# Selective scan: seven of 64 weightings by C moved from VectorE to GpSimd

## What is computed

```python
def _L3_attn_ref(x, norm_w, W_skip, W_in, conv_w, conv_b, Wd1, Wd2, bd2, WB, WC, A_log, W_D, W_out):
    B, L, D = (4, 256, 256)
    E, N, DT, DC = (512, 16, 128, 4)
    ...
    delta = jax.nn.softplus(u @ Wd1.T @ Wd2.T + bd2)
    Bt = u @ WB.T
    Ct = u @ WC.T
    A = -jnp.exp(A_log)

    def step(h, inps):
        d_l, b_l, c_l, u_l = inps
        h = jnp.exp(d_l[..., None] * A) * h + (d_l * u_l)[..., None] * b_l[:, None, :]
        y_l = jnp.einsum('ben,bn->be', h, c_l)
        return (h, y_l)
    ...
    y = (y + u * W_D) * jax.nn.silu(skip)
    return y @ W_out.T
```

## Time and profile before

| what | value |
|---|---|
| median of 3 executions | 1641.8 us (1636.6 to 1643.69) |
| the profiled execution, its own time | 1640.15 us |
| its span, first to last instruction | 1638.8 us |
| busy over the span | PE 1488.8, DVE 1206.6, ACT 895.7, POOL 373.6 us |
| first scan of the loop starts | 1165.06 us |
| last scan of the loop starts | 1387.71 us |
| mean granted TensorE clock | 0.967 |

### The profile page before, as it was taken

The page is one execution under the profiler, slowest core; times in us unless marked ns, Lnnn a source line. Parts: engine busy times, 40 slices in busy tenths (PEclk is TensorE's granted clock), DMA queues, the critical chain, the costliest instruction groups (busy, mean ns, idle before and its releaser), DMA issues.

```text
span 1638.8 us, 16560 instructions
## 1 busy us (share of the span) xinstructions
PE 1488.8 (91%) x5269; PEld 815.9 (50%) x5280; DVE 1206.6 (74%) x1970; ACT 895.7 (55%) x1612; POOL 373.6 (23%) x239
## 2 busy tenths in 40 slices
PE   6898999999799999988999999767888888999998
PEld 2565465478444444344555555333233333467776
DVE  8586587557556367588898988686899999656565
ACT  6444377355323213468888878476766534244443
POOL 1000432241101001000000000020488876023232
PEclk9999999999899999999999999987899999999999
DMA  4001594360300000222121212102000000111110
GB/s 135 1 1 36 228 323 158 83 121 1 154 0 0 0 16 1 66 49 68 26 75 24 75 25 71 59 1 84 0 1 0 1 0 0 55 38 49 55 44 27
DMA packets 45799, 88.19 MB, mean 54 GB/s; under 512 B 10064, under 2 KB 27408, under 8 KB 43408
## 3 DMA queue, kind: packets, MB, share of 16 engines
q1 hardware_dynamic: 40624, 61.42, 12.6%
q0 software_dynamic: 5088, 25.69, 4.3%
HBM read 70.43 MB, written 7.22 MB: 47 GB/s over the span
## 4 chain that ended last, share of the span: by engine, by line
PE 34%; DVE 9%; ACT 6%; issue 4%; POOL 4%; PEldq 1%; DMA 0%; POOLq 0%; DVEq 0%; SPq 0%; ACTq 0%; PEld 0%
PE bank L159 25%; PE bank L3273 3%; POOL s_bu L3168 3%; DVE s_bu L2988 2%; PE bank L2513 2%; DVE s_bu L2983 1%; PE bank L2489 1%; PE bank L3199 1%; DVE g_p L2160 1%; PE bank L2500 1%; DVE g_th L2179 1%; PEldq L147 1%; POOL q_t L2736 1%; PE bank L2488 0%; ACT g_p L2326 0%
## 5 line engine op out<-in xcount | busy, mean ns | idle before, releaser
L3168 POOL TENSOR_TENSOR s_bu<-s_rep,s_du 128x1024 f32<-128x1024 f32 x64 | 150.8, 2361 | 92.8 <-ACT s_rep L3036 54.4
L2983 DVE TENSOR_TENSOR_SCAN s_bu<-bank,s_bu 128x1024 f32<-128x1024 f32 x64 | 146.5, 2288 | 4.7 <-POOL s_bu L3168 2.7
L159 PE MATMUL bank<-e_xs,e_wsp 128*128 128x512 f32 x528 | 127.7, 391 | 0.7 <-issue 0.7
L3273 PE MATMUL bank<-s_bu,ident 128*128 128x512 f32 x256 | 124.7, 610 | 0.7 <-DVE s_dl L2940 0.2
L3052 ACT ACTIVATE bank<-s_dl,s_an 128x510 f32<-128x510 f32 x128 | 82.8, 683 | 53.1 <-DVE s_bu L2983 53.1
L2736 POOL TENSOR_TENSOR q_t<-q_t,q_g 128x704 f32<-128x704 f32 x8 | 13.8, 1720 | 428.9 <-ACT q_t L2781 428.9
L159 PEld LDWEIGHTS bank<-e_xs,e_wsp 128*128 128x128 f32 x528 | 99.1, 188 | 22.7 <-issue 1.9
L159 PE MATMUL bank<-r_am,r_b 128*128 128x512 f32 x240 | 106.0, 592 | 1.4 <-DVE r_am L1783 1.4
L159 PE MATMUL bank<-conditioned,g_wqk 128*128 128x512 f32 x160 | 79.8, 624 | 8.0 <-ACT g_th L2351 7.8
L1849 ACT ACTIVATE r_sl<-bank 128x512 f32<-128x512 f32 x28 | 16.7, 597 | 128.7 <-PE bank L159 128.7
L3383 DVE TENSOR_TENSOR e_s<-e_s,bank 128x512 f32<-128x512 f32 (+1 forms) x50 | 34.3, 686 | 68.8 <-ACT e_s L3515 68.8
(11 more groups left out here) (530 smaller groups left out, 3587.2 us busy)
## 6 DMA issues: line engine op xcount, KB each, us to landing
g_turn<-g_q SPq DMA_DIRECT2D x64, 128.0 KB, 2.3
e_wgu<-in_e_gu SPq DMA_DIRECT2D x22, 256.0 KB, 2.7
b_vw<-b_values SPq DMA_DIRECT2D x48, 64.0 KB, 3.1
e_wd<-in_e_down SPq DMA_DIRECT2D x22, 128.0 KB, 2.6
r_w<-in_r_w SPq DMA_DIRECT2D x3, 896.0 KB, 9.1
g_wqk<-in_g_qk SPq DMA_DIRECT2D x4, 640.0 KB, 4.0
g_wgv<-in_g_gv SPq DMA_DIRECT2D x4, 640.0 KB, 3.9
g_wo<-in_g_wo SPq DMA_DIRECT2D x4, 512.0 KB, 3.9
```

The costliest lines, as they stand in the source:

```text
L159: last = e.matmul(out, lhs, rhs, start=start and n == 0, stop=stop and n == len(pairs) - 1, skip_group_check=True)
L2983: e.tensor_tensor_scan(b, flat(k.pairs[n % 2][:, :, :]), b, 0.0, ALU.mult, ALU.add).then_inc(k["s_scanned"].up(), 1)
L3168: e.tensor_tensor(m.bu[n % m.NBU][:, :, :], m.rep[:, 2 * np:2 * np + 2, :], m.du[:, et, half(h)].unsqueeze(1).to_broadcast([P, 2, HALF]), ...
L3273: summed = e.matmul(banks[6][:, :], k.ident[:, :], m.bu[(n - 1) % m.NBU][:, i, :], start=np == 0 and i == 0, stop=np == m.NP - 1 and i == ...
```

## The change

For the seven jobs in `LATE` (11, 19, 27, 35, 43, 51, 59) VectorE's weighting is left out. ScalarE copies the spread rows of C of that job from `pairs[2]` to an SBUF tile, `kept()` (the space of `s_rs`, [128, 2, 512]), behind decays of the job two further on. GpSimd multiplies `bu` by that tile, in place, behind the input of the job two further on. TensorE's next spread waits for the copy (`spread_free`) and its sum waits for the late weighting (`weighted`).

```diff
+    LATE = [11, 19, 27, 35, 43, 51, 59]
+
+    def kept(self):
+        return self.rs[:, :].rearrange("p (i t) -> p i t", i=2)
+
+    def weighted(self, k, n):
+
+        late = sum(x <= n for x in self.LATE)
+        return k["s_weighted_late"].at(late) if n in self.LATE else k["s_weighted"].at(n + 1 - late)
+
+    def spread_free(self, k, n):
+
+        late = sum(x <= n for x in self.LATE)
+        return k["s_spread_kept"].at(late) if n in self.LATE else k["s_weighted"].at(n + 1 - late)
...
@@ selective_vector
-        if n >= 1:
+        if n >= 1 and n - 1 not in m.LATE:
...
@@ selective_scalar
+        if n - 2 in m.LATE:
+            x = m.LATE.index(n - 2)
+            e.wait_ge(*k["s_spread_c"].at(n - 1))
+            if x:
+                e.wait_ge(*k["s_weighted_late"].at(x))
+            e.copy(flat(m.kept()), flat(k.pairs[2][:, :, :])).then_inc(k["s_spread_kept"].up(), 1)
...
@@ selective_pool
+        if n - 2 in m.LATE:
+            b = m.bu[(n - 2) % m.NBU][:, :, :]
+            e.wait_ge(*k["s_scanned"].at(n - 1))
+            e.wait_ge(*k["s_spread_kept"].at(m.LATE.index(n - 2) + 1))
+            e.tensor_tensor(b, b, m.kept(), ALU.mult).then_inc(k["s_weighted_late"].up(), 1)
...
@@ selective_tensor
-                e.wait_ge(*k["s_weighted"].at(n))
+                e.wait_ge(*m.spread_free(k, n - 1))
...
-            e.wait_ge(*k["s_weighted"].at(n))
+            e.wait_ge(*m.weighted(k, n - 1))
```

## The result

Over seven executions each, the change took 1647.26 us at the median (1645.84 to 1650.85) and the kernel before 1637.81 (1634.78 to 1643.69). The ratio is **1.0056, with a 95% interval of 1.0039 to 1.0074**: slower by 9.2 us, between 6.4 and 12.1. The profiled execution of the change took 1646.19 us with a span of 1644.5, against 1640.15 and 1638.8.

A forecast was written before the change was run, and what follows sets the result against it. VectorE was taken to bound the loop, at GpSimd's pace where GpSimd has no gap. Seven places summed to +7.1 us: 1647.3 from the profiled 1640.15, 1648.9 from the median, forecast 1648.0, range 1640 to 1656.

The forecast's parts named there:

- VectorE bounds the loop, GpSimd's lead decides: Loop: VectorE busy 218.44 of 227 us; cost set by time from GpSimd's input end to scan start, 0.1 to 1.6 us.
- Relief 7.8 us at most, waited away but at job 43: VectorE: seven weightings of 1.11 us removed, 7.8 us at most; job 43 forecast at -0.8 us.
- Copy 1.00, late product 2.36 us: Each late job: ScalarE's copy out of PSUM takes 1.00 us, GpSimd's 128 x 1024 product 2.36 us.
- Copy on ScalarE costs nothing: ScalarE, idle for nearly half of the loop: the seven copies' own time costs nothing; only when they end counts.
- The copy ends behind decays(L+2): ScalarE at late job L: the copy follows decays(L+2); at job 59 it ends near 1379.0, before GpSimd finishes input(61).
- Job 11, +2.3: At scan(14): GpSimd has no lead, so the late product is paid whole, +2.3 us.
- TensorE costed at nothing: TensorE's moved waits for copy and late weighting: 0 us, since it has room, busy 191 of 227 us.
- the second rival: TensorE's clock falls in its new waits, one to seven falls adding 0.7 to 5 us: 1651 us, chance 0.15.
- The first: GpSimd takes the product in its slack, all 7.8 us of VectorE's time come out: 1632.4 us, chance 0.05.
- The third: Shared SBUF read port: each late product holds a scan up 2.3 us, 16 in all: 1663 us, chance 0.03.
- The fourth: It comes out even: lead rebuilt ahead of scans 24 and 38, job 27 caught up by 34: 1640 to 1643, chance 0.15.

The follow-up runs named there:

- e1: The change with GpSimd's late product cut to columns 0 to 15 of each state, copies and waits kept: 188.63 us from scan(8) to scan(63), ratio 1.0003.
- e4: The change with late jobs 11, 27 and 35 only: 199.41 us from scan(8) to scan(63), ratio to the kernel before 1.0040.
- e11: The change with VectorE weighting all 64 jobs again; copies, full-length late products and TensorE's waits kept: 204.61 us from scan(8) to scan(63), ratio 1.0076.
- e3: The kernel before plus seven ScalarE copies and TensorE's next spread waiting for them, no GpSimd product: 192.08 us from scan(8) to scan(63), ratio 1.0002.
- e10: The change with six buffers, late product and its sum one place back, late jobs 16, 36, 41, 44, 57: 188.09 us from scan(8) to scan(63), ratio 0.9975.
- e7: The change, same seven late jobs, with six bu buffers in place of four: 200.21 us from scan(8) to scan(63), ratio 1.0046.
- e9: The change, same seven late jobs, with six buffers, late product and its sum one place back: 200.84 us from scan(8) to scan(63), ratio 1.0049.
- e2: The change with VectorE weighting all 64 jobs, GpSimd multiplying the kept tile by itself, result unused: 197.84 us from scan(8) to scan(63), ratio 1.0040.
- e12: The same kernel as e10, profiled and timed again: 188.49 us from scan(8) to scan(63), ratio to the kernel before 0.9978.
- e6: The kernel before with six bu buffers in place of four: 191.38 us from scan(8) to scan(63), ratio 1.0001.
- e8: The change with six buffers, late product and its sum one place back, late jobs 17, 36, 41, 44, 50, 57: 188.84 us, ratio 0.9978.

## Why the prediction was right

The forecast was +7.1 us, from the profiled execution to 1647.3 and from the median to 1648.9, given as 1648.0. Measured were +9.2 by the ratio (6.4 to 12.1), +7.2 in the loop from scan(8) on, and 1647.26 us. The two totals lie closer than the two differences do, since the kernel before came out lower in the seven runs, 1637.81, than in the three shown; so far the nearness of 1648.0 to 1647.26 is luck. So is some of the agreement of +7.1 with +7.2: job 11 came out 1.6 us cheaper than forecast, and this was made up by 0.8 at scans 30 to 34 and 0.2 to 0.3 each at jobs 19, 51 and 59. I gave the larger chance, 0.55, to a change within 0.5%; 1.0056 lies just outside, and its interval reaches over that bound to both sides.

- **VectorE bounds the loop, GpSimd's lead decides.** Right. e1 shows that GpSimd's 2.3 us are the price, and e4 that they cost by place: 6.6 us at jobs 11, 27 and 35, with the fall behind scan(11) in both profiles. The signs came out as named: scans 14, 22, 30, 38, 46, 54 and 62 all wait for GpSimd's input in the change (2.46, 1.12, 2.44, 2.41, 0.53, 1.13 and 1.14 us), and VectorE's idle time ahead of scans is 17.9 where "some 20" was said.
- **Relief 7.8 us at most, waited away but at job 43.** Right at 19, 27, 35, 43 and 59, by the comparison with e11, and at 11 by that of e4 with e11. At 51 e11's fall hides it.
- **Copy 1.00, late product 2.36 us.** 1.015 and 2.347. **Copy on ScalarE costs nothing** by itself: 0.3 us at most, by e3.
- **The copy ends behind decays(L+2).** Right at jobs 27 and 35, wrong at the other five: there the copy waits 0.22 to 0.48 us more for spread(L), which has to wait for VectorE's weighting(L-1); the prediction left this path out, and at 19, 43, 51 and 59 the product then waits 0.25 or 0.26 us for the copy. At 59 and 51 this is most of the way from -0.2 to +0.1 and from +0.3 to +0.5.
- **Job 11, +2.3.** It was +0.7 against the kernel before, since that one had lost 1.05 us up to scan(14) to a fall of the clock that the change did not have. Against e3, which has no such fall either, it is 1.8; e4, which has it, shows +2.3. The rows that the prediction read at this place come from an execution with the fall: in e3 neither scan(13) nor scan(14) waits, so "no lead" was a mark of that execution and not of the place.
- **TensorE costed at nothing** was wrong by 0.8 against the kernel before, in scans 30 to 34, and by 1.1 against e4. TensorE waited 1.05 us for the late product of job 27, the clock fell (0.66 in 1270 to 1275), the sum took 3.46 us where it takes 1.88, and weighting(30) waited 0.44 for a spread:

```profile
1271.62 3.46 PE L3298 MATMUL bank<-s_bu,ident 128*128 128x512 f32 x4 [1.05 <-POOL s_bu L3194]
...
1275.19 2.29 DVE L2997 TENSOR_TENSOR_SCAN s_bu<-bank,s_bu 128x1024 f32<-128x1024 f32 x1 [2.44 <-POOL s_bu L3188]
...
1281.46 1.22 DVE L3002 TENSOR_TENSOR s_bu<-s_bu,bank 128x1024 f32<-128x1024 f32 x1 [0.44 <-PE bank L3224]
```

In e4 the same wait of 1.05 us was followed by no fall, and the sum took 1.98:

```profile
1271.05 1.98 PE L3298 MATMUL bank<-s_bu,ident 128*128 128x512 f32 x4 [1.05 <-POOL s_bu L3194]
```

With the clock up, then, TensorE's term was rightly nothing. The fall is the second rival, once instead of at seven places, and beside the forecast rather than in its place; the kernel before has one fall in the loop as well. The first (faster, 1632.4) is refuted: the scans waited 17.9 us. The third is refuted as well: scans and weightings kept 2283 and 1196 ns beside 16 us more of GpSimd's work. The Trainium skill's broader sentence (Perfetto Trace Analysis, Optimizing Scalar/DVE Operations) would have let one fear otherwise. By the narrower one of the Trainium skill (SBUF — State Buffer, Who interferes with whom) a VectorE instruction with one input in SBUF, outside the 2-port modes, doesn't contend with GpSimd; these rows agree. The fourth fell at jobs 19 and 35, where the lead was not rebuilt.

What stays open: the timed difference is some 2 us larger than the loop's 7.2, within the interval; no profile shows where, if it is real. Each loop comes from one execution (two for e10's kernel), so how often the clock falls at a place over many executions, and whether the change makes it likelier, is not known.

## What to carry to other kernels

Before work is moved off the busiest engine, read how far ahead the receiving engine is at each place, from the end of its output to the start of its use, and not its share of busy time: with 20% idle over the loop it had between 0.1 and 1.6 us to give where 2.3 were asked. A place costs the moved time, plus what else is queued there, less the lead; the same operation cost 2.3 us at one place and gave 0.7 at another. To keep the relief, buffers, order and places were changed together: more buffers (e7), and more buffers with the new order (e9), gave nothing over the change in the timed runs, and all three gave 0.25% over the kernel before. The good places with the old order and four buffers were not tried. And a lead read from one trace is the lead of that execution: a fall of the clock may have eaten it, as at job 11.

## What the runs showed of the hardware

- A GpSimd product of 128 x 1024 float32 took 1893 ns with the same tile as both operands (e2), 2347 to 2349 with two tiles (the change, e11), and 251 ns with 128 x 32 (e1).
- TensorE's granted clock fell to 0.50 after a wait of 2.47 us (e9), and was 0.66 to 0.67 over the four or five us after waits of 1.05 us (the change, job 27) and 1.86 us (e11). After another wait of 1.86 us, in the change, the sum kept its 1.88 us, and after one of 1.05 us in e4 it took 1.98. So the length of the wait alone doesn't tell whether the clock falls.
- The falls differ between executions of one kernel: one between scan(8) and scan(63) in e12, three in e10. Where two profiles can be compared, a fall cost the loop 0.4 to 1.6 us at a place, and nothing behind scan(11) with six buffers (e6, e8, e10). In e9 the steps behind three falls were 2.1 to 3.1 us longer than before, but there the order differs too.
